# Router logits of a gated attention and mixture-of-experts layer: weights stationary in four column strips, then a second product that adds the halves

## The reference, cut to what matters

```python
x = x + tanh(g_xattn) * xattn(layernorm(x), ctx, mask, Wq, Wkv)
h = layernorm(x)                                   # 2048 x 256
logits = h @ w_router                              # 256 x 8: what the change touches
top_logits, top_idx = top_k(logits, 2)
scores = softmax(top_logits)
for e in range(8):                                 # tokens gathered by expert
    out_e = (silu(proj) * gate) @ fc2_w[e]         # proj, gate = split(rows_e @ fc1_w[e])
shared = (silu(h @ gate_w) * (h @ up_w)) @ down_w
x = x + tanh(g_ffn) * (moe_out + shared)
```

## Time and profile before

| what | us |
|---|---|
| median of 3 runs | 327.98 |
| the three runs | 327.26, 327.98, 331.92 |
| the profiled execution | 332.38 |
| its span, first to last instruction | 330.6 |
| PE busy in it | 306.8 (93%) |
| DVE busy in it | 242.3 (73%) |
| ACT busy in it | 168.8 (51%) |

### The profile page before, as it was taken

How to read it: one execution, slowest core, us unless ns; L and a number is a source line. 1 busy time by engine, 2 the same in 40 slices (tenths; PEclk the granted TensorE clock), 3 DMA queues, 4 the chain that set the end, 5 groups by cost and what they waited for, 6 DMA issues and landing times.

```text
span 330.6 us, 8084 instructions
## 1 busy us (share of the span) xinstructions
PE 306.8 (93%) x2505; PEld 246.1 (74%) x2505; DVE 242.3 (73%) x728; ACT 168.8 (51%) x322; POOL 131.0 (40%) x151
## 2 busy tenths in 40 slices
PE   8948899998989979999999989989999999999996
PEld 8627677887868754665575868778889888888885
DVE  4575597798999994878889977556666667653697
ACT  2443776776777742545693445434444544433240
POOL 5731153232375645133773029953343333432000
PEclk9996999999999996999999999999999999999999
DMA  7892776686656453039237303233233323201943
GB/s 241 248 213 55 234 205 191 174 255 182 205 161 191 141 156 103 2 100 346 104 119 169 82 16 99 73 96 106 90 112 92 98 83 96 79 29 45 428 166 127
DMA packets 34069, 47.18 MB, mean 143 GB/s; under 512 B 5519, under 2 KB 27667, under 8 KB 33522
## 3 DMA queue, kind: packets, MB, share of 16 engines
q1 hardware_dynamic: 28706, 34.61, 35.4%
q0 software_dynamic: 4320, 10.92, 10.0%
q10 hardware_dynamic: 1008, 1.18, 1.2%
HBM read 22.20 MB, written 12.62 MB: 105 GB/s over the span
## 4 chain that ended last, share of the span: by engine, by line
PE 50%; issue 17%; DVE 8%; POOL 8%; DMA 8%; SPq 5%; ACT 1%; DVEq 0%; POOLq 0%; ACTq 0%
PE ps L1760 31%; POOL dispatched L541 4%; PE ps L1589 4%; DMA stacks<-work 4%; DMA expert_rows<-v_s,slot_u 3%; SPq L381 3%; PE ps L1731 2%; PE ps L1808 2%; PE ps L1752 2%; PE ps L1600 2%; PE ps L1449 2%; PE ps L1419 2%; POOL rs L526 2%; SPq L374 1%; DMA x_all<-in_x 1%
## 5 line engine op out<-in xcount | busy, mean ns | idle before, releaser
L597 POOL DMA_INDIRECT expert_rows<-v_s,slot_u x39 | 38.7, 993 | 74.0 <-ACT v_s L866 62.2
L972 DVE TENSOR_REDUCE mx<-ps 128x8 f32<-128x1024 f32 x32 | 39.1, 1223 | 17.3 <-PE ps L1449 17.0
L549 POOL TENSOR_TENSOR work<-work 128x512 bf16<-128x512 f32 x16 | 18.5, 1154 | 51.6 <-ACT work L644 51.5
L675 ACT ACTIVATE probs<-ps 128x1024 f32<-128x1024 f32 x32 | 32.7, 1022 | 10.5 <-PE ps L1482 10.4
L1290 DVE TENSOR_TENSOR act<-ps,sil 128x256 f32<-128x256 f32 x39 | 16.5, 423 | 26.8 <-ACT sil L859 26.7
L859 ACT ACTIVATE sil<-ps 128x256 f32<-128x256 f32 x39 | 15.0, 384 | 41.4 <-PE ps L1760 41.2
L1760 PE MATMUL ps<-fc_hi,xs_hi 128*128 x78 | 34.3, 440 | 0.0
L1760 PE MATMUL ps<-fc_hi,xs_lo 128*128 x78 | 30.8, 395 | 0.0
L866 ACT ACTIVATE v_s<-ps,wt 128x256 f32<-128x256 f32 x39 | 18.5, 474 | 24.1 <-PE ps L1760 24.1
L1760 PE MATMUL ps<-fc_lo,xs_hi 128*128 x78 | 30.7, 394 | 0.0
L1449 PE MATMUL ps<-stacks 96*128 96x128 bf16 x256 | 20.5, 225 | 7.5 <-DMA stacks<-work 3.7
(11 more groups left out here) (221 smaller groups left out, 832.9 us busy)
## 6 DMA issues: line engine op xcount, KB each, us to landing
stacks<-work SPq DMA_DIRECT2D x75, 128.0 KB, 3.1
xs_in<-dispatched SPq DMA_DIRECT2D x39, 129.0 KB, 2.1
fc_s<-in_fc SPq DMA_DIRECT2D x8, 512.0 KB, 4.3
stacks<-work POOLq DMA_DIRECT2D x18, 128.0 KB, 3.4
ctx_s<-in_ctx_t SPq DMA_DIRECT2D x8, 256.0 KB, 3.8
fc_s<-in_fc SPq DMA_DIRECT2D x8, 256.0 KB, 4.9
stacks<-expert_rows SPq DMA_DIRECT2D x2, 1024.0 KB, 6.0
probs<-expert_rows SPq DMA_DIRECT2D x2, 1024.0 KB, 10.1
```

Of the source, the lines that this page charges most:

```text
L549: nc.gpsimd.tensor_tensor(out[:, 2, :], rest, out[:, 1, :], ALU.subtract).then_inc(ready, 1)
L597: nc.gpsimd.indirect_dma_start(ys, bass.IndirectOffsetOnAxis(dst_u[:, r:r + 1], 0), y_out[:, r, :], None, bounds_check=2 * T - 1, oob_is_e ...
L675: nc.scalar.activation(probs[:, 2 * j + h], ps_t, ACT.Exp, scale=HD ** -0.5).then_inc(probs_ok[j][h], 1)
L972: nc.vector.reduce_max(mx[:, j, 8 * h:8 * h + 8], ps_s, AX_X).then_inc(max_ok[j][h], 1)
```

## The change

The router turns its operands round. `wr_s` is widened from 8 to 32 columns (24 of them stay zero) and becomes the stationary operand; 128 tokens are the moving operand. Each of the four products of a group (two tiles, two halves of the features) writes its own strip of 32 partitions of `ps_c`, columns 320 to 447, with no accumulation. A new ACT operation, `strips`, copies this 128 by 128 block to `lg_t` in SBUF (a place that the table uses only later). A new PE product, `router_sum`, takes `lg_t` as stationary operand and a constant 128 by 16 matrix `to_rows` as moving operand: it adds the two halves and turns tokens back to rows, 16 logits of two tiles. DVE makes `to_rows` once from the identity at the start. In DVE's steps `logits` moves from ahead of `pieces(s - 2, 1)` to behind it, and in step s = 9 so also behind `times_0(1)`.

```diff
-NV = 8
+NV = 32
...
+            def strips(g):
+                sa.wait_ge(strips_done, g + 1)
+                if g:
+                    sa.wait_ge(router_done, g)
+                nc.scalar.activation(lg_t[:, :], ps_c[:, 320:320 + P], ACT.Copy).then_inc(strips_ok, 1)
...
                 if live(s - 4):
                     heads_out(s - 4, 1)
+                if live(s - 5):
+                    strips(s - 5)
...
             heads_out(g - 1, 1)
+            strips(g - 2)
             tanh_0(1)
...
             heads_out(g, 1)
+            strips(g - 1)
             second_row(g - 1, 0)
...
             second_row(g, 0)
+            strips(g)
             second_row(g, 1)
...
-                                      ps_c[:, 0:2 * NV].rearrange("p (j e) -> p j e", j=2)[:, :, 0:8]
+                                      ps_c[:, 0:16].rearrange("p (j e) -> p j e", j=2)
...
+            by_strip = ident[:, :].rearrange("p (j k e) -> p j k e", j=2, k=2)
+            link(nc.vector.tensor_tensor(to_rows[:, :, :], by_strip[:, :, 0, 0:8], by_strip[:, :, 1, 0:8], ALU.add))
...
                     maxima(s - 2, 1, 1)
-                if live(s - 4):
-                    logits(s - 4)
                 if live(s - 2):
                     pieces(s - 2, 1)
                 if s == G + 1:
                     times_0(1)
                 if live(s - 4):
+                    logits(s - 4)
                     choice(s - 4)
...
                 for j in range(2):
                     for k in range(2):
-                        last = nc.tensor.matmul(ps_c[:, NV * j:NV * j + NV],
-                                                xt_all[:, k, TG * g + P * j:TG * g + P * j + P], wr_s[:, k, :],
-                                                start=k == 0, stop=k == 1)
-                last.then_inc(router_done, 1)
+                        strip = NV * (2 * j + k)
+                        last = nc.tensor.matmul(ps_c[strip:strip + NV, 320:320 + P], wr_s[:, k, :],
+                                                xt_all[:, k, TG * g + P * j:TG * g + P * j + P], start=True, stop=True)
+                last.then_inc(strips_done, 1)
+
+            def router_sum(g):
+
+                pe.wait_ge(strips_ok, g + 1)
+                nc.tensor.matmul(ps_c[:, 0:16], lg_t[:, :], to_rows[:, :, :].rearrange("p j e -> p (j e)"),
+                                 start=True, stop=True).then_inc(router_done, 1)
...
                     values_t(s - 3, 1)
+                if live(s - 4):
+                    router_sum(s - 4)
...
             values_t(g, 1)
+            router_sum(g - 1)
             shared_0(14)
...
             router(g)
             shared_1(4)
+            router_sum(g)
             shared_1(5)
```

More of the change, by code:

```diff
@@ L103, in build_program @@
         wr_s = sb("wr_s", [P, 2, NV])
+        to_rows = sb("to_rows", [P, 2, 8])
         fc1_s = sb("fc1_s", [P, 2 * E, 2 * FI])
@@ L220, in build_program @@
         hid_1 = v_s[:, :, :, :].rearrange("p a j e -> p (a j) e")
+        lg_t = nc.alloc_sbuf_tensor_at("lg_t", [P, P], F32, offset=start["past"])
         xs_in = nc.alloc_sbuf_tensor_at("xs_in", [P, 4, ROW], F32, offset=start["row_s"])
@@ L267, in build_program @@
             ln2_var0 ln2_var1 rs2_ok0 rs2_ok1 xn2_ok0 xn2_ok1 dup_ok0 dup_ok1
-            x2t_done xt_ok router_done lg_read dif_ok ex_ok oh_ok w_ok pos_done pos_read slots_ok cum_ok
+            x2t_done xt_ok strips_done strips_ok router_done lg_read dif_ok ex_ok oh_ok w_ok pos_done pos_read slots_ok cum_ok
             scat0 scat1 scat_first table_ok words_ok pads_ok pad_out dve_link pool_link
@@ L299, in build_program @@
         rs2_ok, xn2_ok, dup_ok = two("rs2_ok"), two("xn2_ok"), two("dup_ok")
+        strips_done, strips_ok = S["strips_done"], S["strips_ok"]
         x2t_done, xt_ok, router_done, lg_read = S["x2t_done"], S["xt_ok"], S["router_done"], S["lg_read"]
```

## The result

The changed kernel ran at a median of 333.88 us (331.49 to 334.75, six runs) beside 328.06 us for the kernel before (327.26 to 331.92, six runs): a ratio of **1.0118, 95% interval 1.0074 to 1.0163**. Slower, but by less than the 2% that count as a difference here. The ratio is the one on record with its interval; the quotient of the two medians is 1.0177, above that interval; why the two differ so much stays open. Repeated later beside three experiments, the change came out at 1.0095 (1.0055 to 1.0135), which holds the forecast.

What follows compares the result with a forecast made beforehand. Loop bound by query-stack transfers and DVE's maxima, not PE (93% busy); PE never idle from 163 to 189. Step 9's 1.0 plus groups 6 and 7's 1.3 gave 2.3 on 327.98: 330.3 us, range 327.0 to 334.7.

Steps and rivals of the forecast that it cites:

- rival of strips one after the other: Router products run serially, 0.94 us instead of 0.22; three places on the path pay 0.7 more, 332.4 us; chance 0.03.
- PE's time counting: Rival for all eight routers: PE time saved is kernel time, 3.8 us off, 324.2 us; chance 0.13.
- PE's saving: Router on PE, each group: 0.91 us replaced by 0.44, so 0.47 us less PE work.
- The sign "0.22 to 0.35 us" for the router: What a trace should show on PE: a router of eight rows taking 0.22 to 0.35 us.
- strips: New ACT copy of 128 columns out of PSUM: 0.28 us, bounds 0.20 and 0.384.
- Step 9: ACT's strips(5) delays tanh_0(1), and logits stand behind times_0(1); max_t(7, 1) starts at 146.05 instead of 145.09: +1.0 us.
- Groups 6 and 7: Behind the loop, logits come later through router_sum; positions(7) starts at 167.3 instead of 166.05: +1.3 us.
- the loop at nothing: Groups 0 to 5: PE's saving and ACT's copy cost nothing, covered by waits; 1.4 us in all if ACT's cover is gone.
- The half clock: Rival: a half-clock stretch comes in most executions, costing 3.2 to 3.9 us, 333.5 to 334.2 us; chance 0.25.
- Slack, or the loop gives back: Rival: waits have unseen slack, or the loop regains what the end loses; 328.0 us; chance 0.14.

Runs made afterwards that it cites:

- order_alone: Kernel before, old router everywhere, with only DVE's logits copy moved behind the pieces in steps 4 to 8; ratio to before 1.0052 (1.0024 to 1.0081).
- loop_only: Changed kernel with the new router in groups 0 to 4 only; groups 5 to 7 and logits(5) as before; ratio to before 1.0025 (0.9988 to 1.0061).
- tail_only: Changed kernel with the old router in groups 0 to 4, the new one in groups 5 to 7 only; ratio to before 1.0117 (1.0073 to 1.0161).
- best: Changed kernel: old router and DVE order in groups 0 to 4, strips(5), logits(5) put back, tanh_0(3) behind strips(6), shared_1 products ahead of tokens_t(7), positions(7); ratio 1.0013.
- heads_first: Changed kernel with strips(5) behind tanh_0(1), logits(5) ahead of the pieces, and group 6's heads_out and strips ahead of tanh_0(3); ratio to before 1.0071.
- step9_undone: Changed kernel with two step 9 instructions put back: strips(5) behind tanh_0(1), logits(5) ahead of the pieces; ratio to before 1.0065 (1.0028 to 1.0101).

## Why the prediction came out as it did

**The sign and the places were right.** PE's time in the loop is not the kernel's time, step 9 lost by the two named orders, and groups 6 and 7 lost by waiting for the sum. The rival of strips one after the other (0.03, 0.94 us) is refuted by 0.40, that of PE's time counting (0.13) by a longer time with 2.4 us less of PE.

**The terms.** *PE's saving*: 0.47 per group predicted, 0.48 measured, in part by luck: values and strips took 1.30 where the sum had 1.01 + 0.22, the product that adds the halves 0.14 where it had 0.22. (The sign "0.22 to 0.35 us" for the router was just missed: 0.36 to 0.40 from its start to the next operation, waits taken off.) *strips* 0.28, measured 0.27 to 0.29. *Step 9*: +1.0 predicted, 1.20 measured. Against router(5), `gated_0(1)` came 1.01 later (1.04 predicted), and the idle times were those named (3.02 ahead of `gated_0`, 1.68 ahead of `max_t(7, 1)`). The 0.2 lie behind the maxima: the sum put the pieces 1.15 behind the maxima's start, where the logits' copy had stood in the earlier trace rows, and they came 1.31 behind it (143.62 to 144.93). Before, they had come 1.32 behind it too, with the copy between, so that the copy had cost nothing where it stood:

```profile
144.23 0.17 DVE L980 TENSOR_SCALAR mx_pc<-mx 128x16 bf16<-128x16 f32 x1
```

The rest lies between the logits and `max_t`. *Groups 6 and 7*: +1.3 predicted, 1.51 measured. Of it 0.78 had come up by `tokens_t(7)` (164.22 - 161.97, less the 1.47 by which `max_t(7, 1)` was late), where 0.75 was predicted; from there to `positions(7)` it took 4.81 us where the sum had 4.58, in parts of about 0.1 or less. Both terms were right in kind and 0.2 too small, 2.71 for 2.3.

**The step that failed** is the loop at nothing: PE's saving there is costed at nothing, ACT's copy too ("so I cost it at nothing"), and DVE has no term at all. The prediction looked for a cost in ACT's copy (up to 0.28 a step); no run shows one. It said nothing of the logits' move on DVE in steps 4 to 8, though it had the earlier trace rows with DVE busy 13.75 of 14.80 us and charged the same move in step 9. order_alone shows the cost without the new router, 1.0052. With 2.71 from step 9 on and 0.4 to 0.7 in steps 5 to 7 the traces give 3.1 to 3.4 us, a ratio near 1.010, which both intervals of the change hold. How large the loop's share is, and how much of it is this order, its holds, the strips and the sum, stays open within these intervals: loop_only, with all of them, was not slower than order_alone, and tail_only, with none of them in the loop, was not faster than the change.

**The half clock** (0.25) forecast 333.5 to 334.2, and 333.88 lies there; that the range holds the result is owed in part to the room left for this rival, which is luck, since the clock does not tell the two kernels apart. In the second set the mean granted clock was 0.982 for the change and 0.981 for before (one run of 753 us left out), and over the runs that the ratio compares 0.987 and 0.984, so the change was not lowered more. (For the first set only the clocks of the change are on record, 0.979 to 0.990, and that of the profiled execution before, 0.979.) In the first pair of profiles each kernel spent 13.8 us at a granted clock of 0.50: before from 23.4 to 30.3 and from 122.4 to 129.3, the change from 19.5 to 29.8 and from 125.3 to 128.8. The prediction had seen only the second stretch of before. All fourteen profiles hold a stretch between 17 and 32 us, so the assumption that the median run is free of the half clock is not borne out, but it does not explain the difference. The rule named with that rival (the Trainium skill, TensorE: Matmul & The Clock Gate, What's actually happening) would have had the idler PE throttled more: no run here shows it for this change.

**"Slack, or the loop gives back"** (0.14): step 9 did not give back (nothing regained between `max_t(7, 1)` and `positions(7)`, nor with only one edit undone).

## What to carry to other kernels

Price a move on every engine's queue in every step it happens in, not only where the trace shows a wait: the move of a 0.17 us copy that was charged in step 9 also cost time in the loop, by itself, and there it had been left out. An operation can stand in a queue for nothing, in a gap that is there without it too (here the 1.32 us from the maxima to the pieces); moved, it costs its length. Where a helper operation needs a result of another engine, put it behind what can run already (here `tanh_0` ahead of `strips`, logits ahead of the pieces): two swaps took back 1.6 of 2.7 us. And compare two profiles only by stretches that repeat to 0.03 us between kernels that are alike there, from the same event on and not between the same times; a wait for a transfer that one of them shows may be that execution's own.

## What the runs showed of the hardware

Some DVE operations of 0.17 us from SBUF to SBUF were held until a POOL instruction ended, when that had started earlier: the pieces' first operation at 0.39 to 0.50 us in the rows above, the addition to `cum` at 1.17, and in order_alone a cast of 128x8 elements took 1.10 us both times in the loop (0.17 in each such cast of best) and ended with POOL's subtraction, the first time 84.21 with 84.18:

```profile
83.11 1.10 DVE L1071 CAST slot_u<-slot_f 128x8 uint32<-128x8 f32 x1
```

```profile
83.02 1.16 POOL L549 TENSOR_TENSOR work<-work 128x512 bf16<-128x512 f32 x1 [2.43 <-ACT work L644]
```

Copies from PSUM in the same position were not held (0.16 at 106.40, inside POOL's 105.79 to 106.94), and not every operation from SBUF was: in loop_only the sum of the new counts took 0.20 at 115.74, inside POOL's subtraction of 115.71 to 116.87, and the addition behind it, at 115.98, was held to 116.89. The Trainium skill (SBUF — State Buffer, SBUF: two separate sides) states an exclusive lock on a port pair that VectorE and GpSimd share; the trace agrees with it, in that the held one ends with the other. The 0.28 us by which heads_first lost its gain in step 9 look like this too, with an indirect DMA issue of POOL's in the place of the subtraction. But such an issue does not always hold: in step9_undone the same operation started 0.50 us into it (143.39, POOL's 142.89 to 143.86) and took 0.17, in heads_first 0.52 into it (142.38, 141.86) and took 0.46. So a small shift on DVE can move an operation into such a hold (0.93 us for that cast) or out of it.
